# Moving the second layer's output projection and layer norm from a stage of its own into the windowed-attention loop

## The chip, the cores and the metric

One Trainium2 chip, 8 cores, one launch. Each core takes half of one of the four sequences (with a halo), so the cores do the same work on different data and do not talk to each other. The metric is the device time in microseconds (us) of the slowest core.

## The reference, cut to what matters

Two transformer layers, each attention and then a feed-forward part, with the layer norm after each sum. The input is (4, 4096, 1024).

```
x = layernorm(x + L0_attn(x))     # quaternion projections, 16 heads, full softmax attention
x = layernorm(x + L0_ffn(x))      # weights and activations put on an FP6 grid
x = layernorm(x + L1_attn(x))     # 16 heads, 2 kv heads, window of 256: out @ Wo + bo
x = layernorm(x + L1_ffn(x))      # token shift:
    x_prev = x moved by one token, zero in front
    xr = mu_r * x + (1 - mu_r) * x_prev ;  xk = mu_k * x + (1 - mu_k) * x_prev
    out = sigmoid(xr @ W_r) * (relu(xk @ W_k)**2 @ W_v)
```

The change touches the third and the fourth line only.

## The kernel before

**Scheduling.** There is no planner. A small class, `Sched` (line 36), keeps one list of instructions for each engine: `t` TensorE, `v` VectorE, `s` ScalarE, `g` GpSimd, `y` SyncE (SP). `sch.op` and `sch.dma` append to the list and take a list of semaphore waits; `emit` (line 62) writes the waits ahead of the instruction on the same engine, at line 69. So every engine works strictly in the order in which the program was written, and a DMA whose wait is not met holds every later DMA of the same issuing engine. All transposing loads, all stores and a few small loads are issued by SP; weight loads and the loads of the residual are issued by GpSimd. Every VectorE and ScalarE instruction also waits for the one before it.

**Stages.** One core holds SPAN = 2304 tokens, in NSL = 18 slices of 128 tokens, or 6 query tiles of QT = 384 tokens (3 slices each). After layer 0 its result lies in DRAM as `Y2SP` (tokens by features, bf16). Then:

1. *Keys and values of layer 1*: `Y2SP` is read transposed (L1005), projected (L1021), and the values are turned (L1038, bf16 transposes on TensorE).
2. *Windowed attention* (loop over `qt`, 6 query tiles): 8 transposing loads of the tile (L1062), 64 matmuls for the queries (L1078), and then 8 head pairs `hp`. A head pair is 10 score matmuls (L1107) into PSUM "sets" of two banks, 5 exponentials on ScalarE (L1122), 10 mask products on VectorE (L1130), 18 matmuls with the values (L1146), and on VectorE a reciprocal (L1153) and 6 scalings (L1167). The scores rotate over three sets (`par = sg % 3`, banks 0 to 5). At the end of a query tile three stores (L1175) write it to `ATT1` in DRAM. The next tile's L1062 loads stand behind these stores in SP's list.
3. *Output projection and layer norm* (the loop over `sl`, 18 slices; it begins after the last query tile). It loads the weight `W1O` (L1197) and the bias; a slice is then 8 transposing loads from `ATT1` (L1229), a load of the residual (L1238), 16 matmuls (L1254) and 2 for the bias (L1258), 2 sums with the residual (L1268), the row sum (L1275), the squares on ScalarE (L1281), three small instructions on one column (L1284, L1287, L1290), logarithm and exponential (L1295, L1297), the scaling (L1299), and 8 float32 transposes on TensorE (L1309), each copied from PSUM (L1313) into `Y3C`, the feature-major float32 copy in SBUF on which the last stages work.
4. *Receptance* (L1343 to L1392): the two vectors of mixing factors are loaded by SP (L1343, L1345), the weight WRT by GpSimd; 32 one-column copies (L1359) keep the token in front of each of the five token tiles; then for each token tile 8 times a difference and a mix on VectorE (L1368, L1373), 64 matmuls (L1388) and 8 sigmoids (L1392).
5. *Key, value and end* (L1401 to L1533): the same for the keys (for tile 0 L1419 and L1425, for the others four instructions, L1430, L1435, L1439 and L1442, since the first column comes from the kept copy), matmuls (L1458, L1483), the sum into `Y3C`, and for each slice 8 float32 transposes (L1501) into PSUM, a layer norm (L1507 to L1527) and the store.

Of the kernel before, what the change touches and what calls it, by code (L numbers as in the profile page):

```python
# [6 lines left out]
F32 = mybir.dt.float32  # L7
# [25 lines left out]
DMA_SEMS = ("da", "db", "dw0", "dw1", "dw2", "dw3", "dm", "dgm", "dsp", "dy2", "dwd", "dl0", "dl1", "dx0", "dx1", "dxa", "dxb", "dout")  # L33
# [61 lines left out]
def build_program(stage="full"):  # L95
# [24 lines left out]
    Y2SP = nc.dram_tensor("Y2SP", [SPAN, D], BF16, kind="Internal").ap()  # L120
    ATT1 = nc.dram_tensor("ATT1", [SPAN, D], BF16, kind="Internal").ap()
# [7 lines left out]
    with (  # L129
# [54 lines left out]
        def Y3C(c, a, n, dt=F32, p0=0, np_=128):  # L184
            return TY3.bitcast(dt)[p0:p0 + np_, c * (SPAN + 1) + a: c * (SPAN + 1) + a + n]
# [863 lines left out]

        st1 = {"exp_prev": {0: None, 1: None, 2: None}, "pv_norm": None,  # L1050
               "b6_free": None, "atm_free": None, "expt_free": None}
        prev_q_t = None
        for qt in range(NQT):
# [34 lines left out]
            for hp in range(8):  # L1088
                exp_toks = {}
                for sg in range(5):  # L1090
# [3 lines left out]
                    par = sg % 3  # L1094
# [75 lines left out]
                st1["b6_free"] = ntok  # L1170
            sp = None
# [5 lines left out]
            st1["atm_free"] = sp  # L1177
        att1_done = st1["atm_free"]

# [13 lines left out]
        l_w1o = None  # L1193
        for ic in range(8):
            l_w1o = sch.dma("g", "da", (lambda g, s_=W1O[128 * ic:128 * ic + 128, :],
                                        d_=TEV(4096, BF16, 8 * D)[:, ic * D:(ic + 1) * D]:
                                        g.dma_start(out=d_, in_=s_)),  # L1197
                            waits=[tp3_nop, ("dsp", sch.cnt["dsp"]), wdt_done] if ic == 0 else [])
        l_b1o = sch.dma("g", "dgm", lambda g: g.dma_start(out=ROWR[0:1, 0:1024], in_=B1O),
                        waits=[l_idb, tp3_nop])  # L1200
        zc = None
        for c in range(8):
            zc = sch.op("v", (lambda v, c_=c: v.memset(Y3C(c_, 0, 1), 0.0)),
                        waits=[tp3_nop])

        def AF1(p, c, a, n):
            base = (0 + p * 2048) // 2
            return TE[:, base + c * 128 + a: base + c * 128 + a + n]

        af1_free = [None, None]  # L1210
        y2b_free = [None, None]
        y3_done = None
        import os as _os
        _p4cut = int(_os.environ.get("P4CUT", "9"))
        _nsl_p4 = int(stage.split(":")[1]) if stage.startswith("p4b") else NSL
        for sl in range(_nsl_p4):
            p = sl % 2
            dl = "dl0" if p == 0 else "dl1"
            tldA = None
            for c in range(8):  # L1220
                w = []
                if c == 0:
                    w = [("dsp", sch.cnt["dsp"]), tp3_nop]
                    if af1_free[p]:
                        w.append(af1_free[p])
                tldA = sch.dma("y", dl, (lambda y, s_=ATT1[128 * sl:128 * sl + 128,
                                                           128 * c:128 * c + 128],
                                         d_=AF1(p, c, 0, 128):
                                         y.dma_start_transpose(d_, s_)), waits=w)  # L1229
            w = [tp3_nop, ("dy2", 16 * NSL)]  # L1230
            if sl < 2:
                w += [wdt_done, two]
            if y2b_free[p]:
                w.append(y2b_free[p])
            ev_y2 = sch.dma("g", "dx0" if p == 0 else "dx1",
                            (lambda g, d_=TEV(20480 + p * 2048, BF16, 1024),
                             s_=Y2SP[128 * sl:128 * sl + 128, :]:
                             g.dma_start(out=d_, in_=s_)), waits=w)  # L1238
            if _p4cut < 2:
                continue  # L1240
            o_marks = []
            for nh in range(2):
                bank = nh
                last = None
                for ic in range(8):
                    w = []
                    if ic == 0:
                        w = [tldA, l_w1o, l_b1o]
                        if psum_free.get(bank):
                            w.append(psum_free[bank])  # L1250
                    last = sch.op("t", (lambda t, o_=PB(bank, 0, 512),
                                        l_=AF1(p, ic, 0, 128),
                                        r_=TEV(4096, BF16, 8 * D)[:, ic * D + nh * 512: ic * D + nh * 512 + 512],
                                        s0=(ic == 0): t.matmul(o_, l_, r_, start=s0, stop=False)),  # L1254
                                  waits=w)
                last = sch.op("t", (lambda t, o_=PB(bank, 0, 512),
                                    r_=ROWR[0:1, nh * 512:(nh + 1) * 512]:
                                    t.matmul(o_, ONER, r_, start=False, stop=True)), mark=True)  # L1258
                o_marks.append(last)
            af1_free[p] = o_marks[-1]  # L1260
            if _p4cut < 3:
                continue
            ev3 = None
            for nh in range(2):
                ev3 = sch.op("v", (lambda v, d_=TEV(24576, F32, 1024)[:, nh * 512:(nh + 1) * 512],
                                   a_=PB(nh, 0, 512),
                                   b_=TEV(20480 + p * 2048, BF16, 1024)[:, nh * 512:(nh + 1) * 512]:
                                   v.tensor_tensor(d_, a_, b_, ALU.add)),  # L1268
                             waits=[o_marks[nh], ev_y2])
                psum_free[nh] = ev3  # L1270
            y2b_free[p] = ev3
            if _p4cut == 21:
                continue
            zap3 = TEV(24576, F32, 1024)
            t3s = sch.op("v", (lambda v, z_=zap3: v.tensor_scalar(TEV(32768, F32, 1024), z_, 1.0, 0.0,  # L1275
                                                         ALU.mult, ALU.add,
                                                         accum_out=SMALL[:, 70:71])),
                         waits=[ev3])
            if _p4cut == 22:
                continue  # L1280
            t3q = sch.op("s", (lambda ss, z_=zap3: ss.activation(TEV(32768, F32, 1024), z_, AF.Square,  # L1281
                                                        accum_out=SMALL[:, 71:72])),
                         waits=[t3s])
            t3m = sch.op("v", lambda v: v.tensor_scalar(SMALL[:, 72:73], SMALL[:, 70:71],  # L1284
# [8 lines left out]
            if _p4cut == 23:  # L1293
                continue
# [8 lines left out]
            if _p4cut < 4:  # L1303
                continue
# [107 lines left out]
        for ti, (a, n) in enumerate(TILES):  # L1412
# [81 lines left out]
            for ls in range(n // 128):  # L1494
# [35 lines left out]
                for bank in (4, 5, 6, 7):  # L1530
                    psum_free[bank] = t4a
# [74 lines left out]
```

How the kernel before makes its waits and increments, by code:

```python
        def run(engobj, eng):  # L66
            for waits, fn, incsem, incval in self.ops[eng]:
                for (sn, sv) in waits:
                    engobj.wait_ge(sems[sn], sv)
                inst = fn(engobj)
                if incsem is not None:
                    inst.then_inc(sems[incsem], incval)
# [22 lines left out]
def build_program(stage="full"):  # L95
# [287 lines left out]
                8 + sj, n,  # L383
                (lambda ic, s_=sj, n_=n: XSF[128 * ic:128 * ic + 128, 512 * s_:512 * s_ + n_]),
                0, 0,
                (lambda oc, s_=sj, n_=n: QBUF(oc, 512 * s_, n_)))
        if stage == "p1a":
            for c in range(8):
                sch.dma("g", "dout", (lambda g, c_=c, q_=QBUF(c, 0, SPAN): g.dma_start(
                    out=DBG[:, c_ * SPAN: (c_ + 1) * SPAN],
                    in_=q_)), waits=[q_done, k_done])
            sch.op("y", lambda y: y.wait_ge(sem_handles["dout"], sch.cnt["dout"]))
            sch.emit(block, sem_handles)
            stack.close()
            return nc
# [512 lines left out]
            for sl in range(NSL):  # L909
                sch.dma("g", "dout", (lambda gg, sl_=sl: gg.dma_start(
                    out=DBG[:, sl_ * 1024: (sl_ + 1) * 1024],
                    in_=ATT0[128 * sl_:128 * sl_ + 128, :])),
                    waits=[("dsp", sch.cnt["dsp"])])
            sch.op("y", lambda y: y.wait_ge(sem_handles["dout"], sch.cnt["dout"]))
            sch.emit(block, sem_handles)
            stack.close()
```

## Time and profile before

| what | value |
|---|---|
| median of 2 runs | 5448.72 us (5441.09 to 5456.34) |
| the profiled execution | 5442.06 us, its span 5440.5 us |
| spans of the 8 cores | 5418.2 to 5440.5 us |
| TensorE busy | 2824.6 us (52%) |
| ScalarE busy | 1808.7 us (33%) |
| VectorE busy | 1570.3 us (29%) |
| GpSimd busy | 177.8 us (3%) |
| layer 0 and its feed-forward | up to about 3820 us |
| keys and values of layer 1 | 3820 to 3933 us |
| windowed attention | 3933 to 4483 us |
| output projection and layer norm | 4483 to 4827 us |
| receptance | 4827 to 4985 us |
| key, value and end | 4985 to 5440.5 us |

No engine is busy for much over half of the span: the kernel is bound by chains from engine to engine, and a stage has to be read by what ends its waits. Times in the rows are counted from the start of the span. All cores have the same profile within half a per cent, and core 1, the slowest, is shown.

### The profile page before, as it was taken

Reading aid. Unit: us, or ns where it says so; the run is one execution under the profiler, and the core shown is the slowest. Engines: PE = TensorE matmul, PEld = TensorE weight load, DVE = VectorE, ACT = ScalarE, POOL = GpSimd, SP = SyncE. Lnnn points to the kernel's source line nnn. Section 1 sums busy time; section 2 is a strip of 40 time slices with the busy share of each in tenths; the row PEclk is TensorE's granted clock in tenths of the full one; section 3 lists DMA queues with packets and bytes.
Section 4 is the critical chain, followed back from the end, with each engine's and each line's share of the span. In section 5 each row is a group of like instructions: output and inputs, shape, how many; then the busy total and the mean of one; then the engine's idle time right before and its main releaser. Section 6 shows DMA issues by size and latency. Waiting matters only on the chain.

```text
span 5440.5 us, 63668 instructions; the slowest of 8 cores (5418.2 to 5440.5 us)
## 1 busy us (share of the span) xinstructions
PE 2824.6 (52%) x17954; PEld 1425.7 (26%) x17954; DVE 1570.3 (29%) x3498; ACT 1808.7 (33%) x2292; POOL 177.8 (3%) x339
## 2 busy tenths in 40 slices
PE   0255257777776424355555555563265654545434
PEld 0122114444443112132322323231132331212112
DVE  0355310000000123522223232324144443344454
ACT  0022106777774024254544445350022220010000
POOL 0011020000000100000000000000000000000000
PEclk9977576666666755556666666666655656777666
DMA  1322130000001310000000000000300002111000
GB/s 16 72 38 35 39 47 8 4 4 4 4 4 23 50 35 12 23 12 14 10 15 12 11 16 11 17 7 23 66 13 23 14 18 50 31 21 31 27 21 24
DMA packets 174640, 123.34 MB, mean 23 GB/s; under 512 B 106824, under 2 KB 157680, under 8 KB 174320
## 3 DMA queue, kind: packets, MB, share of 16 engines
q0 software_dynamic: 46864, 59.31, 6.6%
q1 hardware_dynamic: 127456, 59.95, 4.1%
q8 instruction: 178, 2.92, 0.2%
q14 instruction: 142, 1.16, 0.1%
HBM read 117.63 MB, written 23.59 MB: 26 GB/s over the span
## 4 chain that ended last, share of the span: by engine, by line
PE 36%; ACT 24%; DVE 16%; issue 9%; DMA 9%; SPq 4%; POOL 1%; DVEq 1%; ACTq 1%; PEldq 0%; POOLq 0%
ACT TE L520 18%; PE PALL L550 10%; PE PALL L508 4%; PE PALL L463 3%; PE PALL L331 2%; PE PALL L1146 2%; PE PALL L796 2%; PE PALL L1254 2%; ACT TE L1122 2%; DMA TY<-XFF 2%; PE PALL L1078 1%; SPq L701 1%; DMA SMALL<-QBI 1%; PE PALL L1388 1%; PE PALL L1458 1%
## 5 line engine op out<-in xcount | busy, mean ns | idle before, releaser
L520 ACT ACTIVATE TE<-PALL,BIASB 128x768 bf16<-128x768 f32 x1536 | 1384.6, 901 | 971.3 <-PE PALL L508 592.1
L508 PE MATMUL PALL<-TY 64*128 64x384 bf16 x3072 | 864.6, 425 | 698.7 <-ACT TE L520 687.0
L508 PEld LDWEIGHTS PALL<-TY 64*128 64x128 bf16 x3072 | 301.2, 98 | 1209.2 <-issue 1131.4
L550 PE MATMUL PALL<-TY,TE 128*128 128x65 bf16 x9216 | 530.3, 242 | 0.0
L550 PEld LDWEIGHTS PALL<-TY,TE 128*128 128x128 bf16 x9216 | 502.3, 131 | 59.8 <-issue 59.8
L557 DVE RECIPROCAL SMALL<-PALL 128x6 f32<-128x6 f32 x48 | 9.4, 196 | 1644.1 <-PE PALL L550 1617.8
L331 PE MATMUL PALL<-TY,TE 128*128 128x512 bf16 (+1 forms) x832 | 205.2, 412 | 378.7 <-DVE TE L297 214.4
L1122 ACT ACTIVATE TE<-PALL,BIASB 128x256 bf16<-128x256 f32 (+2 forms) x240 | 154.9, 645 | 498.2 <-PE PALL L1107 480.2
L463 PE MATMUL PALL<-TE,TY 128*128 128x512 bf16 x512 | 150.1, 446 | 243.5 <-DMA TY<-XFF 243.5
L331 PEld LDWEIGHTS PALL<-TY,TE 128*128 128x128 bf16 x832 | 86.8, 106 | 497.0 <-issue 426.1
L717 PE MATMUL PALL<-TE,TY 128*128 128x512 bf16 x288 | 91.2, 473 | 192.2 <-DMA TY<-ATT 192.1
L1146 PE MATMUL PALL<-TY,TE 128*128 128x65 bf16 x864 | 130.5, 214 | 116.2 <-DVE TE L1130 114.1
L815 ACT ACTIVATE TY<-TY 128x1024 f32<-128x1024 f32 x18 | 19.0, 1057 | 480.6 <-DVE TY L811 480.6
L1510 ACT ACTIVATE PALL<-PALL 128x1024 f32<-128x1024 f32 x18 | 18.2, 1009 | 416.5 <-DVE PALL L1507 416.5
L1130 DVE TENSOR_TENSOR TE<-TE 128x128 bf16<-128x128 bf16 (+2 forms) x480 | 133.6, 278 | 62.6 <-ACT TE L1122 12.4
L1458 PE MATMUL PALL<-TY 128*128 128x512 bf16 (+1 forms) x320 | 73.8, 388 | 139.4 <-DVE TY L1442 107.5
L463 PEld LDWEIGHTS PALL<-TE,TY 128*128 128x128 bf16 x512 | 50.7, 109 | 323.7 <-issue 291.1
L1309 PE MATMUL PALL<-IDF,TE 128*128 128x128 f32 x144 | 64.3, 446 | 135.8 <-DVE TE L1299 116.1
L473 DVE CAST TY<-PALL 128x512 bf16<-128x512 f32 x64 | 44.4, 694 | 305.1 <-PE PALL L467 287.9
L1146 PEld LDWEIGHTS PALL<-TY,TE 128*128 128x128 bf16 x864 | 90.1, 104 | 158.4 <-issue 134.6
L1078 PE MATMUL PALL<-TY 128*128 128x384 bf16 x384 | 76.3, 368 | 91.9 <-DMA TY<-Y2SP 91.8
L1107 PE MATMUL PALL<-TY 64*128 64x128 bf16 (+2 forms) x480 | 114.0, 336 | 18.9 <-DVE TY L1082 6.8
(172 smaller groups left out, 2769.2 us busy)
## 6 DMA issues: line engine op xcount, KB each, us to landing
TY<-XFF POOLq DMA_DIRECT2D x192, 128.0 KB, 4.8
TY<-XST POOLq DMA_DIRECT2D x18, 512.0 KB, 3.9
YOUT<-TE SPq DMA_DIRECT2D x18, 512.0 KB, 2.6
ATT<-TY SPq DMA_DIRECT2D x36, 128.0 KB, 1.8
Y2SP<-TY SPq DMA_DIRECT2D x18, 256.0 KB, 2.0
ATT<-TY SPq DMA_DIRECT2D x18, 256.0 KB, 2.3
TE<-Y2SP POOLq DMA_DIRECT2D x18, 256.0 KB, 3.3
TY<-QW SPq DMA_DIRECT2D x32, 128.0 KB, 2.7
```

What stands on the lines that cost most here:

```text
L331: t.matmul(o_, l_, r_, start=s0, stop=s1)),
L463: s0=(ic == 0): t.matmul(o_, l_, r_, start=s0, stop=False)),
L508: t.matmul(o_, l_, r_, start=True, stop=True, tile_position=tp)),
L520: ss.activation(o_, i_, AF.Exp, bias=BIASB[:, 63:64], scale=0.125)),
L550: t.matmul(o_, l_, r_, start=s0, stop=False, skip_group_check=True)),
L796: s0=(ic == 0): t.matmul(o_, l_, r_, start=s0, stop=False)),
L1078: t.matmul(o_, l_, r_, start=s0, stop=s1)),
L1107: t.matmul(o_, l_, r_, start=True, stop=True, tile_position=tp)),
L1122: ss.activation(o_, i_, AF.Exp, bias=BIASB[:, 60:61], scale=1.0)),
L1130: v.tensor_tensor(d_, d_, m_, ALU.mult)),
L1146: t.matmul(o_, l_, r_, start=s0, stop=False, skip_group_check=True)),
L1458: t.matmul(o_, l_, r_, start=s0, stop=s1)),
```

## The change

The loop of stage 3 becomes a function `p4_slice(sl)`, and `p4_pump(avail, budget)` calls it from inside the attention loop: after every head pair with `avail = 3*qt - 1` and a budget of 1, after the three stores of a query tile with `avail = 3*qt + 2` and a budget of 2, and after the loop until all 18 slices are done. The weight and the bias are loaded ahead of the attention. The scores use two PSUM sets in place of three, so that banks 4 and 5 serve the projection.

A slice no longer transposes on TensorE. It writes its normed rows as bf16 (`Y3B`) and stores them to a new DRAM tensor `Y3SP`; after the last slice SP reads all of it back with 8 transposing loads for each slice into a `Y3C` that is now bf16 and has no zero column in front. The column in front of token 0 is a zeroed column of `SMALL`, so that tile 0 of the receptance and of the keys also takes four VectorE instructions. The transposes of the last stage are bf16, into one PSUM bank.

```diff
+        l_w1o = None
+        for ic in range(8):
+            l_w1o = sch.dma("g", "da", ...W1O -> TEV(24576, BF16, 8 * D)...,
+                            waits=[l_wq1, tp2_nop, p2v_last] if ic == 0 else [])
+        def p4_slice(sl):
+            p = sl % 2
+            for c in range(8):
+                w = []
+                if c == 0:
+                    w = [("dsp", sch.cnt["dsp"])]
+                    if p4s["oproj"].get(sl - 2):
+                        w.append(p4s["oproj"][sl - 2])
+                tldA = sch.dma("y", "dw2" if p == 0 else "dw3", ...ATT1 transposed -> AF1(p, c)..., waits=w)
+            ldy2 = sch.dma("g", ...Y2SP -> TEV(20480 + p * 2048)..., waits=wy)
+            ... 16 + 2 matmuls into banks 4 and 5, 2 sums, row sum ...
+            t3q = sch.op("s", ...Square..., waits=[t3s])
+            t3m = sch.op("v", ...)            # no longer waits for t3q
+            t3m2 = sch.op("v", ...)
+            t3v = sch.op("v", ..., waits=[t3q])
+            t3l, t3e = Ln, Exp on "s"
+            t3a = sch.op("v", (lambda v, y_=Y3B(p): v.tensor_scalar(y_, Z3AP, ...)), waits=wa)
+            p4s["spill"][sl] = sch.dma("y", "dy3", ...Y3B(p) -> Y3SP..., waits=[t3a, spill of sl - 1])
+        def p4_pump(avail, budget):
+            done = 0
+            while done < budget and p4s["n"] < NSL and p4s["n"] <= avail:
+                p4_slice(p4s["n"]); p4s["n"] += 1; done += 1
-                    par = sg % 3
+                    par = sg % 2
...
                 st1["b6_free"] = ntok
+                p4_pump(3 * qt - 1, 1)
             (three stores of the query tile, L1175)
             st1["atm_free"] = sp
+            p4_pump(3 * qt + 2, 2)
         att1_done = st1["atm_free"]
+        p4_pump(NSL, 10 ** 9)
-        (stage 3: the loop over sl, with 8 float32 transposes and 8 copies per slice)
+        for sl in range(NSL):
+            for c in range(8):
+                w = []
+                if c == 0:
+                    w = [("dy3", 16 * (sl + 1)), tp3_nop, st1["pv_norm"]]
+                    if sl >= 2:
+                        w.append(rl_tok[sl - 2])
+                tok = sch.dma("y", dl, ...Y3SP transposed -> Y3C(c, 128 * sl, 128)..., waits=w)
+            rl_tok[sl] = tok
         l_mur, l_muk = the two loads of the mixing factors, on "y" (unchanged, now behind the loop above)
         for ti in range(1, 5):            # kept columns
-                                   waits=[y3_done])
+                                   waits=[rl_tok[(a - 1) // 128]] if c == 0 else [])
         (receptance, tile 0 and the others)
-                            waits=[y3_done, l_muk] + ...
+                            waits=rl_need(ti) + [zc, l_muk] + ...
         (last stage, per slice)
-                                      i_=Y3C(c, 1 + tok0, 128): t.transpose(o_, i_, IDF)),
+                                      i_=Y3C(c, tok0, 128): t.transpose(o_, i_, IDB)),
```

## Rows read from the trace of the kernel before

**Rows 1.** Busy time by stretch: us, PE, PEld, DVE, ACT, POOL (instructions), PEclk, DMA share, GB/s
```profile
3944.70:4483.30 538.60, 320.39 (x1728) 179.26 (x1728) 254.21 (x864) 154.87 (x240) 0.00 (x0) 0.57 0.06 16
4483.30:4826.60 343.30, 171.98 (x468) 63.91 (x468) 117.53 (x328) 29.64 (x72) 18.67 (x35) 0.68 0.19 39
```

**Rows 2.** Waits of the DMA queue of SP, 3900 to 4900 us: total, times, longest
```profile
SPq L69 <- DVE TY L1167: 482.3, 6, 81.4
SPq L69 <- PE PALL L1258: 112.0, 16, 7.5
```

**Rows 3.** Timeline, turn between two query tiles: start, us, engine, line, instruction [idle before]
```profile
4021.22 1.31 SPq L1175 DMA_DIRECT2D ATT<-TY  x3
...
4022.68 9.96 SPq L1062 DMA_TRANSPOSE TY<-Y2SP  x8
...
4034.01 6.23 PE L1078 MATMUL PALL<-TY 128*128 128x384 bf16 x23 [15.59 <-DMA TY<-Y2SP]
```

**Rows 4.** Timeline, end of the attention and first slice of the projection stage
```profile
4483.34 1.30 SPq L1175 DMA_DIRECT2D ATT<-TY  x3
...
4486.99 38.75 SPq L1229 DMA_TRANSPOSE TE<-ATT  x24
...
4509.53 3.57 PE L1254 MATMUL PALL<-TE 128*128 128x512 bf16 x8 [29.38 <-DMA TE<-ATT]
...
4519.63 0.15 DVE L1284 TENSOR_SCALAR SMALL<-SMALL 128x1 f32<-128x1 f32 x1 [1.47 <-ACT TE L1281]
...
4520.15 0.16 DVE L1290 SCALAR_TENSOR_TENSOR SMALL<-SMALL 128x1 f32<-128x1 f32 x1
...
4521.22 0.81 DVE L1299 TENSOR_SCALAR TE<-TE,SMALL 128x1024 f32<-128x1024 f32 x1 [0.92 <-ACT SMALL L1297]
```

**Rows 5.** Timeline, the same kind of slice interleaved with layer 0's attention
```profile
3113.16 9.79 SPq L701 DMA_TRANSPOSE TY<-ATT  x8
...
3124.32 3.40 PE L717 MATMUL PALL<-TE,TY 128*128 128x512 bf16 x8 [17.20 <-DMA TY<-ATT]
...
3148.36 0.33 SPq L837 DMA_DIRECT2D Y2SP<-TY  x1
...
3148.86 9.79 SPq L701 DMA_TRANSPOSE TY<-ATT  x8
```

**Rows 6.** Timeline, end of one head pair and the start of the next
```profile
4461.57 2.27 PE L1146 MATMUL PALL<-TY,TE 128*128 128x65 bf16 x16 [0.71 <-DVE TE L1130]
...
4464.52 3.60 ACT L1122 ACTIVATE TE<-PALL,BIASB 128x256 bf16<-128x256 f32 x5 [4.65 <-PE PALL L1107]
...
4467.08 3.72 DVE L1130 TENSOR_TENSOR TE<-TE 128x128 bf16<-128x128 bf16 x10
```

**Rows 7.** Transposing loads by line: ns min/median/max of the issue on SP
```profile
L701 SPq DMA_TRANSPOSE TY<-ATT x144: 1079/1202/1425, 2257.7 to 3756.7; - x144
...
L1062 SPq DMA_TRANSPOSE TY<-Y2SP x48: 1098/1221/1229, 3933.3 to 4400.7; - x48
```

**Rows 8.** Timeline of SP alone, 4486 to 4505 us, while W1O is being loaded
```profile
4486.99 19.09 SPq L1229 DMA_TRANSPOSE TE<-ATT  x13
```

**Rows 9.** Timeline, the mixing factors and the first difference of the receptance
```profile
4782.50 0.50 SPq L1343 DMA_DIRECT2D BIASB<-MUR  x1
...
4784.28 0.33 SPq L1345 DMA_DIRECT2D BIASB<-MUK  x1
...
4826.65 0.69 DVE L1368 TENSOR_TENSOR TE<-TY 128x512 f32<-128x512 f32 x1 [0.17 <-DVE SMALL L1359]
```

**Rows 10.** Groups from 3500 us on: line, engine, shapes, count | busy us, mean ns | idle before
```profile
L1501 PE MATMUL PALL<-IDF,TY 128*128 128x128 f32 x144 | 61.0, 424 | 110.1 <-DVE TE L1527 81.9 <-DVE TY L1491 9.4
...
L1368 DVE TENSOR_TENSOR TE<-TY 128x512 f32<-128x512 f32 x32 | 22.2, 692 | 56.1 <-PEq L1396 49.6 <-DVE TY L1373 6.3 <-DVE SMALL L1359 0.2
...
L1442 DVE SCALAR_TENSOR_TENSOR TY<-TE,BIASB,SMALL 128x1 bf16<-128x1 f32 x32 | 7.1, 222 | 3.7 <-DVE TY L1439 0.5
...
L1435 DVE TENSOR_TENSOR TE<-TY,SMALL 128x1 f32<-128x1 f32 x32 | 5.1, 159 | 3.7 <-DVE TE L1430 0.5
...
L1038 PE MATMUL PALL<-IDB,TY 128*128 128x128 bf16 x18 | 4.5, 252 | 5.4 <-PE PALL L1038 3.4 <-DVE TY L1029 1.0 <-DVE TY L1045 0.8
```

More of the change, by code:

```diff
@@ L1048, in build_program @@
             vt_done = ev
+        l_w1o = None
+        for ic in range(8):
+            l_w1o = sch.dma("g", "da", (lambda g, s_=W1O[128 * ic:128 * ic + 128, :],
+                                        d_=TEV(24576, BF16, 8 * D)[:, ic * D:(ic + 1) * D]:
+                                        g.dma_start(out=d_, in_=s_)),
+                            waits=[l_wq1, tp2_nop, p2v_last] if ic == 0 else [])
+        l_b1o = sch.dma("g", "dgm", lambda g: g.dma_start(out=ROWR[0:1, 0:1024], in_=B1O),
+                        waits=[t_fbrow, tp2_nop, p2v_last])
@@ L1191, in build_program @@
         tp3_nop = sch.op("t", lambda t: t.nop(), mark=True)
[L1193 to L1219, printed above, removed]
+        zc = sch.op("v", lambda v: v.memset(SMALL[:, 166:167], 0.0))
+        rl_tok = {}
+        for sl in range(NSL):
+            dl = "dl0" if sl % 2 == 0 else "dl1"
+            tok = None
             for c in range(8):
@@ L1231, in build_program @@
[L1231 to L1283, printed above, removed]
@@ new lines, in build_program @@
+                    if sl >= 2:
+                        w.append(rl_tok[sl - 2])
+                tok = sch.dma("y", dl, (lambda y, d_=Y3C(c, 128 * sl, 128),
+                                        s_=Y3SP[128 * sl:128 * sl + 128,
+                                                128 * c:128 * c + 128]:
+                                        y.dma_start_transpose(d_, s_)), waits=w)
+            rl_tok[sl] = tok
+        if stage == "p4":
+            for sl in range(NSL):
+                sch.dma("g", "dout", (lambda gg, sl_=sl: gg.dma_start(
+                    out=DBG[:, sl_ * 1024: (sl_ + 1) * 1024],
+                    in_=Y3SP[128 * sl_:128 * sl_ + 128, :])),
+                    waits=[("dy3", 16 * NSL)])
@@ L1529, in build_program @@
                              waits=[t4e, y4_free[0]] if y4_free[0] else [t4e])
-                for bank in (4, 5, 6, 7):
+                for bank in (4, 5):
                     psum_free[bank] = t4a
```

248 lines of the change are left out of this document (141 added, 107 removed).

## The prediction

> **What bounds the kernel now.** I read the stretches first [rows 1]. In the windowed attention (538.6 us) TensorE is busy for 320.39 us, VectorE for 254.21, ScalarE for 154.87; in the projection stage (343.3 us) TensorE 171.98, VectorE 117.53, ScalarE 29.64. Nothing is full, so on paper the second stage fits into the holes of the first. The waits of SP's queue come next [rows 2]: SP waited 482.3 us in 6 waits for the last scaling of a query tile (L1167), and in the projection stage 112.0 us in 16 waits for the bias matmul. The reader is to see that one unmet wait holds the whole queue: what stands behind it is not issued. Third, the timeline where one query tile turns into the next [rows 3]: stores at 4021.22, behind them eight transposing loads, first query matmul at 4034.01, 12.79 us later, after 15.59 us in which TensorE stood idle. That is the price of one group of eight transposing loads when nothing covers it. Earlier in the kernel the same pattern stands: eight loads issued at 3113.16, first matmul at 3124.32, 11.16 us [rows 5]. By line, one such load takes 1202 or 1221 ns of SP [rows 7], eight of them 9.79 us, so a pitch of 1.225 us.
>
> **Where the 18 slices go.** The pump's arithmetic: after tile 0 it emits slices 0 and 1, after head pair 0 of tile 1 slice 2, then 3 and 4 after tile 1, and so on. So a *pair* stands at each of 5 turns between tiles, a *single* behind head pair 0 of 5 tiles, and slices 15, 16 and 17 come behind the last tile.
>
> **A pair at a turn.** SP's order becomes: stores of the tile, 8 loads of slice A, store of A (waits for its scaling), 8 loads of slice B, store of B, 8 loads of the next tile's queries. Each waits for the end of the slice ahead, so nothing overlaps. From the first store of the tile:
> - the loads of A wait until the stores have landed: 4486.99 - 4483.34 = 3.65 us [rows 4];
> - loads to first matmul 11.16 us [rows 5]: 14.8;
> - first matmul to the end of the scaling: 4509.53 to 4521.22 + 0.81 is 12.50 us [rows 4], less about 0.5, since L1284 and L1287 no longer wait for the squares (4520.15 - 4519.63): 12.0, in all 26.8;
> - scaling to the store 0.1, store to the next load 0.5 (3148.36 to 3148.86 [rows 5]): 27.4;
> - B: 11.16 + 12.0 + 0.6: 51.2;
> - the query loads: 4034.01 - 4022.68 = 11.33 [rows 3]: 62.5.
>
> Before it was 12.79. A turn costs 49.7 us more, 5 turns 248.5. That is 24.9 us for a slice, where the stage of its own needed 343.3 / 18 = 19.1 [rows 1].
>
> **A single behind head pair 0.** Its loads stand behind the query loads and are covered by the 64 query matmuls and the head pair. Its chain isn't: in program order VectorE and ScalarE do the whole slice before the masks and exponentials of head pair 1. TensorE ends the head pair at 4461.57 + 2.27 = 4463.84, and the next masks began at 4467.08 [rows 6]; now they begin 12.0 + 0.1 after 4463.84, at 4475.9, or 8.9 us later. 5 of them: 44.5. The first eight matmuls took 3.57 us [rows 4], after a long idle time; here TensorE has just worked and may be quicker: I take 7 us each as the floor.
>
> **Two score sets.** The exponentials of sets 2 to 4 now wait for the one two back. In a usual head pair ScalarE starts at 4464.52 and is done after 3.60 us, at 4468.1, while the masks run from 4467.08 to 4470.8 [rows 6]: the masks follow the scalings, and a slip of half a microsecond in the exponentials is covered. The cover is missing only in the first head pair of a tile, 6 times about 0.5: 3 us. Below, 0; above, 0.4 in each of the 42 others, 17 more.
>
> **The tail.** After slice 16 at 51.2, slice 17 takes 11.16 + 12.0 + 0.6: the read-back begins at 75.0 us. It is 144 transposing loads of 1.225 us, 176.4 us, on one queue. While GpSimd loads the receptance weight beside them it is slower: with W1O in flight 13 took 19.09 us [rows 8], 1.47 each, 3.2 us over the pitch. So 254.6. One might stop at 128 loads, since the kept columns need slice 15. But the two small loads L1343 and L1345 stand behind all 144 in SP's list, and the first difference waits for the second: 1.8 us apart [rows 9], and about 2 to land (an estimate: the last of the stores of [rows 4] was issued some 0.9 us after the first and had landed at 3.65): 258.4. Before, the same distance was 4826.65 - 4483.34 = 343.3 [rows 4, 9]. The tail wins 84.9 us.
>
> At this place a rule of the Trainium skill speaks against me. Advanced Engine Details and Errata, section X-Bar Transpose (TRN2), says that transposing DMAs are as fast as regular ones. The rows disagree for SP's issue: three plain stores take 1.30 us [rows 4], 0.43 each, against 1.2 for a transposing load. What the rule would make of the time is a rival below.
>
> **Small parts.** *W1O loaded early* meets the key and value loads; with it in flight 13 loads lost 3.2 us [rows 8]: +3 (0 to 8). *Tile 0 with four instructions*: 159 + 222 ns and a gap of 0.12 each [rows 10], about 0.65 for each of 8 chunks in two stages, both with TensorE waiting: +10.4. *bf16 transposes at the end*: 424 against 252 ns [rows 10], chained, 144 of them: 24.8, and something of the gap: -26. They stand in a serial chain, so this counts. Below, 0.05 more each, 32; above, 18, if the gap grows. *Reading a bf16 `Y3C`*: no row shows a difference with bf16 in and float32 out. The floor is the 692 ns of L1368 [rows 10] halved in all 80 differences, 28 us less; the other bound is no gain. I take no gain, since the result stays float32, as in that row. *Removed* transposes and copies are already in the tail's 343.3. *Weight loads for the receptance* lie under the read-back.
>
> **The sum.** 248.5 + 44.5 + 3 - 84.9 + 3 + 10.4 - 26 = +198.5 us. Against the profiled execution's 5442.06 that is 5640.6; the median of the runs, 5448.7, lies 6.7 above it. I say 5643.
>
> **Rivals.**
> 1. *The read-back runs slower than its pitch*, as with W1O in flight, 1.47 us for all 144: 144 x 0.245 less the 3.2 counted, +32, so 5675. For it: other loads are in flight at its start, and no row has more than 16 such loads back to back. Against it: [rows 7] has a narrow spread.
> 2. *The turns overlap*: if SP did not hold later loads behind a store's wait, B's loads and the query loads would run under A's chain. A's first matmul at 14.8, both chains done by 38.8, queries ready at about 36, so a turn costs 26 less. 5 turns are 130, the tail 23 less: 5643 - 153 = 5490, within 2%. Against it stand [rows 2], and the loads at 3148.86 [rows 5], issued only behind the store.
> 3. *Transposing loads as cheap as plain ones*, the other side. At 0.43 us a group of eight needs 5.4 instead of 11.16; 13 uncovered groups save 74, the read-back 144 x 0.8 = 114. 5643 - 188 = 5455, no difference; the sum falls under +2% once the issue takes under about 0.84 us. This is the skill's rule above taken as a mechanism. [Rows 7] has a minimum of 1079 ns over 144, so it is nearly excluded.
> 4. *The interleave fills the holes as meant* (singles and turns hidden by neighbours, only the read-back paid): 198.5 - 248.5 - 44.5 = -94.5, so 5643 - 293 = 5350, faster by 1.8%; a little over 2% if something of the read-back hides too. It needs independent work behind each wait in each engine's list; there is none at a turn.
>
> **Chances.** Forecast as worked out 0.70; rival 1 or several prices high at once 0.16; between the forecast and rival 2 (a part of the turns overlaps, still over +2%) 0.07; rivals 2 and 3, within 2%, 0.05; rival 4, faster, 0.02. A difference of 2% is about what a measurement of this kernel can tell from no change. So faster 0.02, same 0.05, slower 0.93. Low end: singles at 7 (-9.5), faster chains by 1 us in 13 slices (-13), no early-load cost (-3), transposes -6, half of the floor for bf16 reads -14: 5597, and I go to 5590. High end: read-back +32, two sets +17, early load +5, less gain at the end +8: 5705.
>
> **What would show it.** At each turn between tiles TensorE should have three idle stretches that end in a DMA, with 62 to 63 us from the store to the first query matmul; SP's list should show store, 8 loads, store, 8 loads. SP should then issue 144 transposing loads in a row in 176 to 180 us, and the receptance should begin only behind the load of MUK. Head pair 1 of tiles 1 to 5 should start its masks about 9 us late, and the other head pairs keep their 8 us. I am wrong if the query matmuls begin under 45 us after the store, or if the read-back is much shorter than 170 us.

## The result, and the profile after

| | before | after |
|---|---|---|
| median of the runs | 5446.01 us (8 runs, 5435.09 to 5462.33) | 5681.78 us (9 runs, 5671.41 to 5705.81) |
| the profiled execution, span | 5440.5 us (core 1) | 5670.1 us (core 6) |
| TensorE, VectorE, ScalarE busy | 2824.6, 1570.3, 1808.7 us | 2727.7, 1533.2, 1807.2 us |

The kernel is slower: the ratio after to before is 1.043, 95% interval 1.041 to 1.045. VectorE has 37 us less to do and TensorE about 76 us less (core 1 in both traces, 2824.6 against 2748.9; the 2727.7 of core 6 in the table lacks the records of 81 matmuls), and the span is 229.6 us longer. Work went away and waits came. The granted TensorE clock is no rival: its mean over the attention stretch, between the two levels of 1.2 and 2.4 GHz, is 0.57 of full speed before and 0.60 after.

Where the time went, read in both timelines as distances between the same events (core 1 before, core 6 after; the two cores reach the first of them, the last store of `Y2SP`, 4.6 us apart, after being the earlier; the prediction's parts are put beside the stretches they fall into):

| stretch | before, us | after, us | difference | predicted |
|---|---|---|---|---|
| start to the last store of `Y2SP` | 3824.3 | 3819.7 | -4.6 | 0 |
| last store of `Y2SP` to the first query load | 108.95 | 126.06 | +17.1 | +3 |
| first query load to the first store of the last query tile | 550.05 | 856.63 | +306.6 | +296 |
| that store to the first difference of the receptance | 343.3 | 267.8 | -75.5 | -84.9 |
| first difference of the receptance to that of the keys | 158.6 | 163.6 | +5.0 | +5.2 |
| from there to the end | 455.3 | 436.3 | -19.0 | -20.8 |
| sum | | | +229.6 | +198.5 |

The second row depends on the cores that are compared. From the last store of `Y2SP` to the first query load the eight cores need 108.7 to 112.5 us before and 122.5 to 126.1 after, so the mean difference is +12.4 and not +17.1. For the two stretches behind it the means give +306.4 and -75.4, as in the table.

**The turn between two query tiles.** Timeline of the kernel after, SP's queue alone; the columns are start, us, engine, line, instruction, count. It answers [rows 3]. L1286 stores the query tile, L1086 loads a slice of the projection, L1151 stores it, L1172 loads the queries.

```profile
4187.59 1.30 SPq L1286 DMA_DIRECT2D ATT<-TY  x3
4191.13 10.01 SPq L1086 DMA_TRANSPOSE TY<-ATT  x8
4215.72 0.33 SPq L1151 DMA_DIRECT2D Y3SP<-TY  x1
4216.20 10.03 SPq L1086 DMA_TRANSPOSE TY<-ATT  x8
4240.22 0.33 SPq L1151 DMA_DIRECT2D Y3SP<-TY  x1
4240.70 10.21 SPq L1172 DMA_TRANSPOSE TY<-Y2SP  x8
4251.05 11.03 SPq L1086 DMA_TRANSPOSE TY<-ATT  x8
4284.65 0.33 SPq L1151 DMA_DIRECT2D Y3SP<-TY  x1
```

The reader is to see the holes: SP ends eight loads at 4201.14 and issues nothing until the store at 4215.72, 14.6 us later, because the store stands in the list ahead of the loads that could go. The same stretch, all engines:

```profile
4203.07 3.19 PE L1104 MATMUL PALL<-TE,TY 128*128 128x512 bf16 x7 [18.70 <-DMA TY<-ATT]
...
4214.77 0.81 DVE L1143 TENSOR_SCALAR TY<-TE,SMALL 128x1024 bf16<-128x1024 f32 x1 [0.98 <-ACT SMALL L1138]
...
4227.82 3.57 PE L1104 MATMUL PALL<-TE,TY 128*128 128x512 bf16 x8 [17.94 <-DMA TY<-ATT]
...
4239.27 0.81 DVE L1143 TENSOR_SCALAR TY<-TE,SMALL 128x1024 bf16<-128x1024 f32 x1 [0.98 <-ACT SMALL L1138]
...
4252.29 12.38 PE L1188 MATMUL PALL<-TY 128*128 128x384 bf16 x64 [17.91 <-DMA TY<-Y2SP]
...
4269.77 2.28 PE L1256 MATMUL PALL<-TY,TE 128*128 128x65 bf16 x16 [0.45 <-DVE TE L1240]
...
4272.65 3.19 PE L1104 MATMUL PALL<-TE,TY 128*128 128x512 bf16 x7 [0.61 <-DVE SMALL L1263]
...
4283.72 0.81 DVE L1143 TENSOR_SCALAR TY<-TE,SMALL 128x1024 bf16<-128x1024 f32 x1 [0.98 <-ACT SMALL L1138]
4284.63 3.72 DVE L1240 TENSOR_TENSOR TE<-TE 128x128 bf16<-128x128 bf16 x10
```

Three idle stretches of TensorE of 18 us, each ended by a DMA, and the query matmuls 64.70 us after the store at 4187.59. In the lines with x7 the record of the first of eight matmuls is missing; it began about 0.4 us earlier. The last four lines are the single behind head pair 0: its matmuls start at once, since its loads came long before, and yet head pair 1 gets its masks only at 4284.63, behind the slice's scaling, 12.6 us after TensorE ended the head pair at 4272.05; [rows 6] has 3.2.

**The read-back.** Timeline of the kernel after, SP alone and then the first difference of the receptance on VectorE; it answers [rows 9].

```profile
4878.95 0.33 SPq L1151 DMA_DIRECT2D Y3SP<-TY  x1
4879.50 186.50 SPq L1320 DMA_TRANSPOSE TY<-Y3SP  x144
5066.11 0.51 SPq L1336 DMA_DIRECT2D BIASB<-MUR  x1
5068.08 0.33 SPq L1338 DMA_DIRECT2D BIASB<-MUK  x1
```

```profile
5070.24 0.69 DVE L1367 TENSOR_TENSOR TE<-TY 128x511 f32<-128x511 bf16 x1 [21.71 <-DMA BIASB<-MUK]
```

144 loads in a row take 186.5 us, 3.3% of the span, in which TensorE and ScalarE do nothing and VectorE works for 4.9 us, and the wait of VectorE ends in the load of MUK, as the order of the list says.

### The profile page after: what moved, and what is told of

The parts are those of the page before. It is cut to its first block, busy times and chain, and to the rows that moved or that the text cites. A ratio compares the mean times of both kernels' runs of the same rounds, so it can differ in the third digit from the quotient of the medians.

```text
span 5670.1 us, 62959 instructions; the slowest of 8 cores (5649.9 to 5670.1 us)
## 1 busy us (share of the span) xinstructions
PE 2727.7 (48%) x17729; PEld 1392.0 (25%) x17810; DVE 1533.2 (27%) x3379; ACT 1807.2 (32%) x2292; POOL 177.8 (3%) x339
## 4 chain that ended last, share of the span: by engine, by line
PE 33%; ACT 22%; DVE 16%; DMA 9%; issue 9%; SPq 8%; POOL 1%; DVEq 1%; ACTq 1%; PEldq 0%; POOLq 0%
ACT TE L521 17%; PE PALL L551 9%; PE PALL L509 4%; SPq L1320 3%; PE PALL L464 3%; PE PALL L332 2%; SPq L1086 2%; PE PALL L1256 2%; PE PALL L797 2%; PE PALL L1104 2%; DMA TY<-XFF 2%; PE PALL L1188 1%; PE PALL L1463 1%; DMA SMALL<-QBI 1%; DVE TE L1240 1%
## 5 line engine op out<-in xcount | busy, mean ns | idle before, releaser
L551 PEld LDWEIGHTS PALL<-TY,TE 128*128 128x128 bf16 x9216 | 501.8, 131 | 59.9 <-issue 59.9
L464 PE MATMUL PALL<-TE,TY 128*128 128x512 bf16 x500 | 147.5, 444 | 247.8 <-DMA TY<-XFF 247.0
L1104 PE MATMUL PALL<-TE,TY 128*128 128x512 bf16 x276 | 97.7, 516 | 241.7 <-DMA TY<-ATT 238.7
L332 PEld LDWEIGHTS PALL<-TY,TE 128*128 128x128 bf16 x832 | 86.2, 106 | 493.3 <-issue 421.4
L1403 PE MATMUL PALL<-TY 128*128 128x512 bf16 (+1 forms) x315 | 71.5, 391 | 271.9 <-DVE TY L1379 215.7
L718 PE MATMUL PALL<-TE,TY 128*128 128x512 bf16 x271 | 86.2, 468 | 198.4 <-DMA TY<-ATT 125.0
L1240 DVE TENSOR_TENSOR TE<-TE 128x128 bf16<-128x128 bf16 (+2 forms) x480 | 133.7, 278 | 62.0 <-ACT TE L1232 12.6
L1124 ACT ACTIVATE TE<-TE 128x1024 f32<-128x1024 f32 x18 | 19.0, 1056 | 402.4 <-DVE TE L1120 390.6
L1516 ACT ACTIVATE TY<-PALL 128x1024 f32<-128x1024 bf16 x18 | 18.4, 1023 | 398.1 <-DVE TY L1513 398.1
L1463 PE MATMUL PALL<-TY 128*128 128x512 bf16 (+1 forms) x312 | 75.0, 398 | 145.5 <-DVE TY L1447 144.0
```

The lines of the kernel that those rows point to most:

```text
L332: t.matmul(o_, l_, r_, start=s0, stop=s1)),
L551: t.matmul(o_, l_, r_, start=s0, stop=False, skip_group_check=True)),
L1240: v.tensor_tensor(d_, d_, m_, ALU.mult)),
L1463: t.matmul(o_, l_, r_, start=s0, stop=s1)),
```

## The experiments

Each ran beside the kernel before on the same chip; ratios are to that kernel before, with their 95% intervals. The runs used three chips, on which the median of the kernel before was 5451.9 us (e1 to e4), 5459.8 (e5 to e8) and 5448.1 (e9, e10), so a difference in us between runs of different groups is good to some 10 us. Three groups: which part costs what, what makes the slices cost so much, and what the interleave is worth once it is mended.

### e1: the weight W1O loaded behind the key and value stage

```diff
-                            waits=[l_wq1, tp2_nop, p2v_last] if ic == 0 else [])
+                            waits=[l_wq1, tp2_nop, p2v_last, vt_done] if ic == 0 else [])
```

> One edit to the changed kernel: the loads of W1O and its bias (and, behind them in GpSimd's list, the first residual loads) wait until the keys and values are done, so they fall into the first tile's attention. Theory (the early weight load slowed the transposing loads of the key and value stage): from the last store of Y2SP to the first load of the query tile goes from 126.1 us back to about 109 us, and the whole is 15 to 18 us faster (ratio to the kernel before about 1.040 in place of 1.043). Rival (that stage is longer for another reason, for instance the state of the queues after layer 0): it stays at 120 us or more and the time does not move.

Measured 5670.97 us, ratio 1.039 (1.036 to 1.043). In the kernel after, some of the 40 key and value loads were slow, as the row of the line shows (ns min/median/max of the issue, and time to landing); the second fence is the same of the kernel before:

```profile
L1006 SPq DMA_TRANSPOSE TY<-Y2SP x40: 1106/1261/5658, 3836.9 to 3929.3; - x40
...
DMA to landing us min/median/max: 2.3/2.7/18.4
```

```profile
L1005 SPq DMA_TRANSPOSE TY<-Y2SP x40: 1089/1230/1257, 3839.8 to 3916.8; - x40
...
DMA to landing us min/median/max: 2.3/2.7/5.1
```

A single load took up to 5.66 us to issue and up to 18.4 us to land. All the slow ones are among the first eight, beside which W1O is on its way (SP alone, kernel after, then kernel before):

```profile
3836.90 22.77 SPq L1006 DMA_TRANSPOSE TY<-Y2SP  x8
```

```profile
3839.82 10.02 SPq L1005 DMA_TRANSPOSE TY<-Y2SP  x8
```

In e1 the stage is as short as it was before, 3936.84 - 3827.77 = 109.1 us (SP alone):

```profile
3827.77 0.33 SPq L838 DMA_DIRECT2D Y2SP<-TY  x1
...
3842.88 78.83 SPq L1006 DMA_TRANSPOSE TY<-Y2SP  x40
3936.84 19.34 SPq L1172 DMA_TRANSPOSE TY<-Y2SP  x8
```

But the weight is now fetched from 3937.30 on, and the eight query loads that stand beside it take 19.34 us in place of 10.17. So the longer stage does come from the moved loads meeting transposing loads (the edit holds back the bias and the first residual loads of GpSimd too, so W1O alone was not isolated), and at the next transposing loads about 9 us are paid again. As means of the eight cores, the stage is 12.8 us shorter and the attention 8.6 us longer. The 15 to 18 us expected for the whole did not come: the intervals of e1 and of the kernel after overlap. e8 below moves the weight to where no transposing load is: there the stage is back at 111.0 us, as before, and the attention is not longer than in e3 (691.6 against 692.0).

### e2: the mixing factors loaded ahead of the read-back

```diff
+        l_mur, l_muk = the two loads of the mixing factors, on "y"
         for sl in range(NSL):             # the read-back
-        l_mur, l_muk = ...
```

> One edit to the changed kernel: the two small loads of the mixing factors stand ahead of the 144 transposing loads of the read-back in SP's list. Theory (the receptance waits for them only because of their place in the list): VectorE's first difference then waits for the kept columns, that is for slice 15, and comes about 18 to 20 us earlier, at 248 us after the first store of the last tile in place of 267.8. Rival (the read-back's own end is what is waited for): no change. In both the read-back itself keeps its 186 us.

One run, 5661.87 us, so no interval; the reading is the trace's. VectorE, first the kept columns, then the first difference:

```profile
5053.99 1.96 DVE L1357 CAST SMALL<-TY 128x1 f32<-128x1 bf16 x8 [39.17 <-DMA TY<-Y3SP]
5056.47 0.69 DVE L1367 TENSOR_TENSOR TE<-TY 128x511 f32<-128x511 bf16 x1 [0.53 <-DMA TY<-Y3SP]
```

From the store of the last query tile (4806.57) to the first difference are 249.9 us, against 267.8 of the kernel after. The small loads had cost 18 us by standing last in the list, and only 18, since the next thing that holds the first difference is the last kept column, which needs slice 15 of 18.

### e7: as e2, and the kept columns copied behind the receptance

```diff
-        stash_tok = None                  # 32 one-column copies, ahead of the receptance
-        for ti in range(1, 5): ...
+        (the same 32 copies, behind the receptance and ahead of the keys)
```

> Two edits to the changed kernel: the mixing factors ahead of the read-back, and the 32 copies of the kept columns behind the receptance in place of ahead of it. The read-back keeps its 144 loads. Theory (with the two false orders gone the read-back is only waited for by what needs it): the first difference comes with slice 3, about 125 us after the first store of the last tile in place of 267.8; then the receptance is paced by the loads, 41 us for a tile of four slices, and ends about 295 us after that store in place of 414: about 115 to 120 us faster, a ratio of about 1.021. Rival (VectorE is held by something else ahead of the receptance): less than 30 us faster.

5564.13 us, ratio 1.021 (1.018 to 1.023). The first difference now comes 4930.10 - 4806.72 = 123.4 us after the store of the last query tile:

```profile
4930.10 0.69 DVE L1360 TENSOR_TENSOR TE<-TY 128x511 f32<-128x511 bf16 x1 [46.71 <-DMA TY<-Y3SP]
```

The next token tiles begin at 4972.17, 5013.28 and 5055.62, a pace of 41 to 42 us, that of 32 transposing loads at 1.29. So the read-back still sets the time, but the receptance runs under it. Two false orders, small loads behind a long list and small copies ahead of independent work, were worth 118 us of the 236.

### e6: the read-back in 40 wide loads in place of 144

```diff
-        for sl in range(NSL):             # 8 loads of 128 rows x 128 columns each
+        for ti, (a, n) in enumerate([(0, 512), (512, 512), (1024, 512), (1536, 512), (2048, 256)]):
+            # 8 loads of n rows x 128 columns each
```

> One edit to the changed kernel: the read-back of Y3SP is 40 transposing loads of up to 512 rows by 128 columns in place of 144 of 128 by 128; the same bytes. Theory (a transposing load costs SP 1.25 us whatever its size, and this sets the read-back): 186.6 us fall to about 50 to 55, the whole is about 133 us faster, a ratio of 1.018 to 1.020. Rival (the read-back is bound by the transposed bytes): the loads take 3 to 4 times as long to land, the read-back keeps 150 us or more, a ratio of 1.036 or more.

5563.11 us, ratio 1.019 (1.017 to 1.021). SP alone, and the row of the line:

```profile
4907.99 59.47 SPq L1319 DMA_TRANSPOSE TY<-Y3SP  x40
```

```profile
L1319 SPq DMA_TRANSPOSE TY<-Y3SP x40: 1087/1231/5805, 4908.0 to 4966.3; - x40
```

The same 4.7 MB are back in 59.5 us on this core (3), where the kernel after needs 181.9, and in 58.6 in place of 184.0 as means of the eight cores. On cores of the same kind (the issue time differs a little from core to core, see the last section) the median issue is 1231 ns with 512 rows and 1202 with 128: SP pays for each load, hardly for its bytes. That holds where no weight load is under way. Beside the receptance weight the first eight wide loads took 18.43 us, 17.2 as the mean of the cores, where the next eight took 10.15:

```profile
4907.99 18.43 SPq L1319 DMA_TRANSPOSE TY<-Y3SP  x8
```

In the kernel after, beside the same weight, the first 16 loads of 128 rows took only 0.7 us more than 16 later ones (20.8 against 20.1).

### e4: the kernel before with two score sets

```diff
-                    par = sg % 3
+                    par = sg % 2
```

> One edit to the kernel before: two score sets in place of three in the windowed attention. Theory: the masks follow the scalings of the head pair ahead, so the exponentials have slack; 0 to +3 us, a ratio of 1.000 to 1.001. Rival (score matmuls now wait for exponentials in every head pair and delay the values): 0.4 to 1 us in each of 48 head pairs, +20 to +48 us, a ratio of 1.004 to 1.009.

5453.63 us, ratio 0.999 (0.997 to 1.001). The attention stretch keeps its 550.2 us (mean of the cores, with and without the third set). The third set was worth nothing that can be measured; the prediction had +3, with 0 as its lower bound.

### e3: singles only, none at the turns

```diff
-                p4_pump(3 * qt - 1, 1)
+                if hp in (0, 2, 4):
+                    p4_pump(3 * qt - 1, 1)
...
-            p4_pump(3 * qt + 2, 2)
```

> One edit to the changed kernel: no slice at the turn between two query tiles; slices come behind head pairs 0, 2 and 4 of the next tile, so 15 of the 18 are singles and the last three follow the last tile. Theory (a slice at a turn costs 25.9 us because SP's loads, the layer norm and the store of each are in series, a single only 9.3, its chain on VectorE and ScalarE): five turns fall from 64.7 to 12.8 us each, ten more singles at 9.3 us: 5 x 51.9 - 10 x 9.3 = 166 us faster, a ratio to the kernel before of about 1.012. Rival (the cost of a slice is that of its work on the engines, wherever it is put): about no change, or under 50 us.

5521.43 us, ratio 1.012 (1.008 to 1.017). SP and the first query matmul at a turn:

```profile
4284.56 1.30 SPq L1287 DMA_DIRECT2D ATT<-TY  x3
4286.01 10.19 SPq L1172 DMA_TRANSPOSE TY<-Y2SP  x8
```

```profile
4297.62 2.72 PE L1188 MATMUL PALL<-TY 128*128 128x384 bf16 x8 [16.27 <-DMA TY<-Y2SP]
```

The turn is back at 4297.62 - 4284.56 = 13.1 us, as in [rows 3]. Ten slices moved out of the turns, where each cost 26 us, to places where the loads are covered and about 9 or 10 us of chain are not (the attention of e3 is 141.8 us longer than before for 15 singles, 9.5 each); by the medians this gives 160 us, 166 were expected. The same functions, the same instructions and the same number of transfers: only the place in the lists differs.

### e5: the turns kept, their loads issued ahead of their stores

```diff
+            n0 = p4s["n"]
+            p4_load(n0)
+            p4_load(n0 + 1)
+            if qt + 1 < NQT:
+                qc_next = q_load(qt + 1, prev_q_t)
             p4_pump(3 * qt + 2, 2)        # its slices find their loads done
```

> The changed kernel with the same slices at the same places; only SP's order at a turn is new: the loads of slice A, of slice B and of the next query tile stand together ahead of the two stores. Theory (a turn takes 64.7 us because each group of loads is held behind the store of the slice ahead): the 24 loads run in a row from 3.5 to 33.6 us after the first store, B's matmuls start when they land and A's banks are free, and the first query matmul comes at about 36 to 38 us; 5 x 27 us plus about 12 in the tail, 140 to 155 us faster, a ratio to the kernel before of 1.015 to 1.018. Rival (the chain of sums, layer norm and matmuls of the two slices is the turn): under 40 us gained, a ratio of 1.036 or more.

5538.25 us, ratio 1.015 (1.013 to 1.017). SP, and TensorE under it:

```profile
4536.36 1.36 SPq L1297 DMA_DIRECT2D ATT<-TY  x3
4539.89 19.74 SPq L1086 DMA_TRANSPOSE TY<-ATT  x16
4559.78 10.54 SPq L1177 DMA_TRANSPOSE TY<-Y2SP  x8
4570.47 2.85 SPq L1157 DMA_DIRECT2D Y3SP<-TY  x2
```

```profile
4551.29 3.57 PE L1110 MATMUL PALL<-TE,TY 128*128 128x512 bf16 x8 [18.50 <-DMA TY<-ATT]
...
4561.43 1.89 PE L1110 MATMUL PALL<-TE,TY 128*128 128x512 bf16 x8 [3.26 <-DVE SMALL L1135]
...
4572.65 7.66 PE L1199 MATMUL PALL<-TY 128*128 128x384 bf16 x34 [6.65 <-DMA TY<-Y2SP]
```

The turn takes 4572.65 - 4536.36 = 36.3 us in place of 64.7, with nothing changed but the order of SP's list (the residual loads in GpSimd's list move up with it). Both chains now run under the 24 loads, and what is left of the turn is SP's issuing: 3.5 us until the tile has landed, 24 loads of 1.27 (30.4), and 2.3 to land. This is the number that rival 2 had for a turn, 62.5 - 26 = 36.5.

### e8: all the repairs together

The edits of e3, e6 and e7, and W1O loaded when the first tile's queries are done, beside no transposing load.

> The changed kernel with all repairs together: W1O loaded once the first tile's queries are there, slices behind head pairs 0, 2 and 4 and none at a turn, mixing factors ahead, read-back by 40 wide loads, kept columns copied behind the receptance. Theory (the parts add up): 166 us by the singles, 17 by the weight, and about 170 in the tail, since the first difference comes about 90 us after the first store of the last tile in place of 267.8: 350 us faster than the changed kernel, a ratio to the kernel before of 0.977 to 0.981. Rival (the gains overlap, or the wide loads hold other transfers up): above 0.99.

5348.73 us, ratio 0.980 (0.978 to 0.983), as expected: 333 us under the kernel after and about 107 under the kernel before.

### e10: the same repairs, with the projection as a stage of its own

All 18 slices behind the attention, as before the change, each with its loads two slices ahead of its store.

> The kernel with all repairs, but with all 18 slices behind the attention as a stage of their own, as in the kernel before; the loads are issued two slices ahead and the matmuls of the next slice may run under the layer norm of this one. Theory (the interleave was not what could be won; loads, matmuls and norm in series were the cost, and now SP's 8 loads of 1.25 us are the longest step of a slice): the stage takes 15 + 18 x 10.5 = about 204 us where the kernel before needed 343, and the attention its 550 us again: 0.974 to 0.980, as fast as the interleaved kernel with all repairs or slightly faster. Rival (the interleave does win something that a stage of its own can't): 0.99 or more.

5328.1 us, ratio 0.977 (0.973 to 0.981). The intervals of e8 and e10 overlap: with the loads mended everywhere, the interleave with whole slices gives nothing that can be seen. In the stage of its own the loads set the pace, 10.6 us a slice (SP alone, three stores of slices):

```profile
4522.16 0.51 SPq L1155 DMA_DIRECT2D Y3SP<-TY  x1
4522.83 9.80 SPq L1077 DMA_TRANSPOSE TY<-ATT  x8
4532.78 0.45 SPq L1155 DMA_DIRECT2D Y3SP<-TY  x1
4533.39 9.82 SPq L1077 DMA_TRANSPOSE TY<-ATT  x8
4543.38 0.44 SPq L1155 DMA_DIRECT2D Y3SP<-TY  x1
```

which is about what a single in the loop costs.

### e9: each slice cut into steps over four head pairs

e8, but a slice's first half of the matmuls, its second half with the first sum, its statistics, and its scaling with the store go to four head pairs, each step between the masks and the value matmuls; the loads stand at the start of the tile and behind head pair 2.

```diff
+        def p4_hook(qt, hp):              # called between masks and value matmuls
+            b = 3 * (qt - 1)              # (returns at once for tile 0)
+            for i in range(3):
+                if hp == 2 * i + 3: p4_fin(b + i)
+                if hp == 2 * i + 2: p4_ev(b + i, 1); p4_stats(b + i)
+            for i in range(3):
+                if hp == 2 * i: p4_pe(b + i, 0)
+                if hp == 2 * i + 1: p4_pe(b + i, 1); p4_ev(b + i, 0)
+            if hp == 2: p4_load(b + 2)
```

> The kernel with all repairs, and each slice cut into steps over four head pairs: half of the matmuls, then the other half and a sum, then the second sum, the row sum and the squares, then logarithm, exponential and scaling; each step stands between the scores and the value matmuls of a head pair, so that no engine waits for a step of the same head pair but for the last three. Theory (a single costs 9.3 us because its whole chain stands in front of the next masks; its own work on VectorE is 4.6 us, and part of it fits under the value matmuls): a slice costs 3 to 5 us, 15 x 5 = 75 us less, and 24 less in the tail, where the loads of slices 16 and 17 are issued ahead; a ratio to the kernel before of 0.960 to 0.966. Rival (the matmuls between scores and values delay the head pair as much as the chain did): no more than 30 us under the kernel with all repairs, 0.975 or more.

5226.82 us, ratio 0.957 (0.952 to 0.962): faster than both kernels, by 4.3% and by 8%, and slightly better than the 0.960 to 0.966 expected. A slice's matmuls now run beside the masks:

```profile
4079.07 3.19 PE L1097 MATMUL PALL<-TE,TY 128*128 128x512 bf16 x8 [0.18 <-DVE TY L1325]
4079.12 3.72 DVE L1287 TENSOR_TENSOR TE<-TE 128x128 bf16<-128x128 bf16 x10
```

and the pace of a tile with its three slices is 104 us, as the query loads of two tiles in a row show (4146.11 - 4042.13 = 104.0; a tile without slices takes 92.8 in the kernel before, from the loads at 4022.68 of [rows 3] to the next ones at 4115.51):

```profile
4042.13 10.19 SPq L1208 DMA_TRANSPOSE TY<-Y2SP  x8
...
4146.11 10.20 SPq L1208 DMA_TRANSPOSE TY<-Y2SP  x8
```

By this pair a slice costs (104.0 - 92.8) / 3 = 3.7 us; over the whole attention stretch and all cores it is (611.5 - 550.2) / 15 = 4.1 us. So a slice costs about 4 us in the loop when its chain is cut, about 9 when it is whole, and 26 at a turn. Of what e9 wins over e8, 80 us lie in the attention (691.6 to 611.5), and 30 in the stretch behind it (100.1 to 69.8, from the first store of the last tile to the first difference), where the loads of the last slices are issued ahead.

## Why the prediction was right, and where it missed

The forecast was 5643 us, the range 5590 to 5705; the median is 5681.8, inside the range and 39 us above the forecast. Against the profiled execution the sum was 31 us short (229.6 - 198.5).

- **The pair at a turn** was read rightly: SP holds what stands behind a waiting store. Its steps from the first store are 3.5, 15.5, 28.0, 28.6, 40.2, 53.1, 64.7 us where the prediction had 3.65, 14.8, 26.8, 27.4, 38.6, 51.2, 62.5. Each step was a little short. By the complete records of all cores, eight loads to the first matmul took 11.4 us for slice A and 11.6 for B, where it took 11.16 from the interleaved slices of layer 0, and the chain from the first matmul to the end of the scaling took 12.9 for A and 12.3 for B, not 12.0 (the 15.5 for A's first matmul, read from the lines above, is 0.4 late for the missing record). A turn cost 51.9 in place of 49.7, five of them +11 us. e3 and e5 show that the hold is the cause of what a turn costs: both remove it, one by taking the slices away from the turn and one by the order of the list alone.
- **The single** was right: 9.3 us in place of 8.9, five of them 47. Its mechanism, a whole chain in program order between two head pairs, is borne out by e9 against e8, where the chain is cut: in the attention 80 us less for 15 slices, 9.4 us a slice down to 4.1. The loads of e9 also stand a little earlier; that part was not taken apart.
- **Two score sets**: 3 us predicted, none measured (e4), and the attention stretch of the kernel after is explained without them: 5 x 51.9 + 5 x 9.3 = 306, measured 306.6.
- **The tail**: predicted -84.9, measured -75.5. The first turn of this stretch repeats that of above; the read-back began 77.1 us after the store and not 75.0. The term that was mis-sized is the pitch of the read-back: 186.5 / 144 = 1.295 us, not 1.225 with 3.2 us on top, 6.9 us more. Two things make it up. First, 9.79 / 8 is not a pitch: it leaves out the gap behind the eighth load, and the first load of a group is short. Within a group the pitch on core 1 is 1.244 us, before and after, and each eighth load of the read-back, after which SP has a wait, is followed 1.46 us after its start. Second, the loads of core 1 are compared with those of core 6, where a load takes about 30 ns longer in the kernel before too (median 1232 ns against the 1202 of [rows 7]; the lines are core 6 before and core 1 after):

```profile
L701 SPq DMA_TRANSPOSE TY<-ATT x144: 1094/1232/1364, 2243.9 to 3745.2; - x144
```

```profile
L1320 SPq DMA_TRANSPOSE TY<-Y3SP x144: 1077/1202/2107, 4881.2 to 5062.8; - x144
```

  On core 1 the read-back takes 182.7 us where the prediction had 179.6. Rival 1 had 1.47 us for all 144; the truth lies between, nearer to the forecast. The receptance weight beside it is a small part only: 40 loads long after it, from 4929.36 on, took 51.69 us, 1.29 each.
- **W1O loaded early**: this is the step that failed by most, in size: +3 predicted, +17.1 measured between the cores shown and +12.4 as the mean of all, and the bound of 8 didn't hold it. I had priced it by one row ([rows 8], 13 loads that lost 3.2 us) as if every meeting cost the same. From the first to the last of its 40 loads, their waits included, the stage took 93.65 us where the kernel before needed 78.18, 15.5 more, and most of it in the first eight: 22.77 in place of 10.02, single ones up to 5.66 us, and TensorE waits for them. [Rows 8] has loads of 128 rows, this stage has loads of 512, and what the record shows goes with that size: beside a 2 MB weight 16 loads of 128 rows lost 0.7 us (the read-back of the kernel after) and 1.2 (the projection stage of the kernel before; 3.0 on core 1, the one of [rows 8]), 8 of 384 rows 6.3 (e1), 8 of 512 rows 7.1 (e6) and 11.8 (here), as means of the cores. e6 against the kernel after changes only the size of the loads, and with it their number, beside the same weight. e1 shows that the cost goes along with the weight and the loads behind it, e8 that it is gone where no transposing load is near.
- **The Trainium skill's rule** of X-Bar transposes as fast as regular DMAs (Advanced Engine Details and Errata, section X-Bar Transpose (TRN2)) was weighed as rival 3. The rows of after and of e6 stand against it for SP's issue: 144 loads with a median issue of 1232 ns and 40 loads of up to four times the size at 1231, against 0.33 and 0.43 us for plain stores.
- **Small parts**: tile 0 with four instructions cost +5.0 in the receptance (5.2). At the end the bf16 transposes took 252 ns each, as forecast, and the stretch is 19.0 shorter against 20.8. Reading `Y3C` as bf16 gained nothing, as taken: the difference with bf16 in and float32 out still takes 692 ns. End stage, kernel after, by line and shape (count, busy us, mean ns, idle before); it answers [rows 10]:

```profile
L1506 PE MATMUL PALL<-IDB,TY 128*128 128x128 bf16 x144 | 36.2, 252 | 109.4 <-DVE TE L1533 81.2 <-DVE TY L1496 9.2 <-PE PALL L1506 4.0
...
L1435 DVE TENSOR_TENSOR TE<-TY 128x511 f32<-128x511 bf16 x32 | 22.1, 692 | 41.2 <-DMA TY<-WKT 27.1 <-DMA YOUT<-TE 8.3 <-DVE TY L1447 5.1
```

- **Rival 4**, the interleave that fills the holes, 5350 us by the prediction: not what this change does, but e8 came to 5349 and e9 under it. The number agrees, not the way: e8 reaches it only with the tail mended too, and e10 reaches it without any interleave.

What stays open: why wide transposing loads beside a weight load take four times their usual issue and more, and why a load costs SP some 30 ns more on four of the cores. Neither was taken apart.

## What to carry to other kernels

Before work is moved into another loop to fill holes, write down for each engine's list, SP's too, what stands behind every new wait: here the same slices cost 26, 9 or 4 us each, depending only on where their instructions stood, and loads belong ahead of the stores that wait. A whole dependent chain put between two steps of a loop isn't hidden by it; cut it so that each step finds its input done. And look behind a long list of DMAs for a small load or copy that everything waits for: two of them cost 118 us here, more than even the well cut interleave won over the stage of its own (5328 - 5227 = 101 us, on one chip).

## What the runs showed of the hardware that was not expected

- A transposing load costs SP nearly the same whatever its size, while no weight load is under way: medians on cores 1 and 3 are 1202 ns with 128 rows of 128 columns, 1222 with 384 and 1231 with 512. 40 wide loads brought back in 59.5 us what 144 brought in 181.9 on the same core.
- Beside a 2 MB weight load that GpSimd issued, the cost goes with the size: 8 loads of 512 rows took 21.9 us in the kernel after and 17.2 in e6 in place of 10.1, 8 of 384 rows took 16.4 in e1 in place of 10.1, and 16 of 128 rows 20.8 in place of 20.1 (means of the eight cores). Single ones took up to 5.66 us to issue and up to 18.4 us to land on the core shown (5.1 at most without the weight).
- The issue time of a transposing load differs between cores, the same in both kernels: 1232 ns at the median on cores 0, 2, 4 and 6 and 1202 on cores 1, 3, 5 and 7, for the same 144 loads of layer 0. A difference of 30 ns between two runs is read on the same core or not at all.
